# Two of ten first-activation rows of each chunk carried over through DRAM instead of computed again

## What is computed

```
h = jax.nn.relu(_bn(_conv1x1(x, w_pw1), ...)) * mask_dilate
h = h * vector[:, :, None, None]
h = jax.nn.relu(_bn(_dwconv3x3(h, w_dw), ...)) * mask
h = h * vector[:, :, None, None]
h = _bn(_conv1x1(h, w_pw2), ...) * mask
return x + h
```

## Time and profile before

| | |
|---|---|
| median of 3 runs | 1687.53 us (1687.25 to 1690.31) |
| span of the profiled execution, first to last instruction | 1685.9 us |
| TensorE busy | 1588.0 us (94% of the span) |
| ACT busy | 1270.4 us (75%) |
| DVE busy | 1194.2 us (71%) |
| last stage | from 1169.5 us on |
| one chunk of the last stage | 41.0 us |

### The profile page before, as it was taken

How to read it: one execution, slowest core, us unless ns; L and a number is a source line. 1 busy time by engine, 2 the same in 40 slices (tenths; PEclk the granted TensorE clock), 3 DMA queues, 4 the chain that set the end, 5 groups by cost and what they waited for, 6 DMA issues and landing times. The chain is left out here.

```text
span 1685.9 us, 57844 instructions
## 1 busy us (share of the span) xinstructions
PE 1588.0 (94%) x24130; PEld 1254.3 (74%) x24130; DVE 1194.2 (71%) x1993; ACT 1270.4 (75%) x2405; POOL 110.6 (7%) x189
## 2 busy tenths in 40 slices
PE   6999999999999999999999979466999999999996
PEld 5999999999999999999999953114444444454443
DVE  5777777777777777777777758775766666666664
ACT  5888888888888888888888867663666666666663
POOL 4000000000000000000000000000000000000000
PEclk9999999999999999999999999775999999999998
DMA  6656666656666566666666659860134444334334
GB/s 147 166 160 165 171 169 165 164 161 170 169 166 167 160 167 168 165 174 172 164 166 170 170 196 383 326 247 18 43 83 85 88 81 92 81 81 89 83 83 91
DMA packets 96008, 251.53 MB, mean 149 GB/s; under 512 B 22920, under 2 KB 28956, under 8 KB 95772
## 3 DMA queue, kind: packets, MB, share of 16 engines
q1 hardware_dynamic: 84344, 213.56, 43.5%
q0 software_dynamic: 10880, 35.40, 10.6%
q10 hardware_dynamic: 644, 0.49, 0.2%
HBM read 120.74 MB, written 78.79 MB: 118 GB/s over the span
## 5 line engine op out<-in xcount | busy, mean ns | idle before, releaser
L319 PE MATMUL gates<-state,w_high 64*128 64x384 f32 x4608 | 505.9, 338 | 0.0
L319 PEld LDWEIGHTS gates<-state,w_high 64*128 64x128 f32 x4608 | 417.9, 185 | 0.0
L1263 PE MATMUL psd<-shared 32*32 32x384 f32 x10368 | 296.4, 491 | 0.6 <-issue 0.6
L319 PE MATMUL gates<-state,w_low 64*128 64x384 f32 x2304 | 268.3, 338 | 0.0
L1263 PEld LDWEIGHTS psd<-shared 32*32 32x32 f32 x10368 | 164.8, 103 | 131.1 <-issue 77.3
L319 PE MATMUL gates<-x_both,w_high 64*128 64x384 f32 x2304 | 237.3, 338 | 13.8 <-ACT w_high L373 13.8
L378 ACT ACTIVATE sig_f<-gates 48x384 f32<-48x384 f32 x384 | 187.0, 487 | 46.7 <-PE gates L319 41.2
L319 PEld LDWEIGHTS gates<-x_both,w_high 64*128 64x128 f32 x2304 | 207.5, 186 | 13.8 <-ACT w_high L373 13.8
L319 PEld LDWEIGHTS gates<-state,w_low 64*128 64x128 f32 x2304 | 209.4, 186 | 0.0
L1504 DVE SCALAR_TENSOR_TENSOR acc<-shared,acc 128x768 f32<-128x768 f32 x144 | 146.5, 1018 | 75.5 <-ACT acc L1412 71.7
L474 DVE TENSOR_TENSOR h_new<-sig_o,tanh_c 128x384 f32<-128x384 f32 x192 | 107.2, 559 | 122.3 <-ACT tanh_c L396 122.3
(11 more groups left out here) (166 smaller groups left out, 1626.5 us busy)
## 6 DMA issues: line engine op xcount, KB each, us to landing
x_taps<-x_both SPq DMA_DIRECT2D x192, 195.5 KB, 3.2
x_raw<-x_steps SPq DMA_DIRECT2D x192, 192.0 KB, 3.2
h_rows<-h_new SPq DMA_DIRECT2D x136, 192.0 KB, 2.7
h_in<-h_rows SPq DMA_DIRECT2D x34, 768.0 KB, 6.3
x_last<-x_both SPq DMA_DIRECT2D x192, 98.0 KB, 3.0
shared<-x_parts SPq DMA_DIRECT2D x24, 768.0 KB, 9.4
out<-z POOLq DMA_DIRECT2D x47, 336.0 KB, 5.4
x_parts<-x_lanes POOLq DMA_DIRECT2D x48, 288.0 KB, 4.2
```

The source lines that it names most:

```text
L319: return nc.tensor.matmul(gates[p][d][:, m, 0:NH], w[own, n, m, :], moving[own], start=start, stop=stop)
L1263: mm = nc.tensor.matmul(psd[lane:lane + 32, 2 * x + i, 0:NH], wt[own, to:to + 32], h1p[2 * (s % 2) + x][own, dy + 4 * m:dy + 4 * m + 4, dx ...
```

## The change

Each chunk but the first computes eight new rows, in two jobs of four rows. The first two rows of its `h1` come from the chunk before: once a chunk's rows are there, ACT's queue stores its last two rows into a DRAM tensor `halos` (`save`), and when the next chunk's buffer is free, ACT's queue loads them into its first two rows (`back`). The three pairs move as one DMA for two images, the three DVE units as one each: six saves and six loads a chunk, 11 times. New waits: the first taps of a pair on TensorE and `product` on ACT wait for the load (`halo_back`); a load waits for the save (`halo_saved`) and for the buffer; a later `keep` waits until the rows that it overwrites are saved.

```diff
         def span(c, r):
-            first, last = CH * c - 1 + 5 * r, CH * c + 4 + 5 * r
-            lo, hi = max(first, 0), min(last, H)
-            return lo, hi, 5 * r + lo - first
+            lo = CH * c + 1 + 4 * r if c or r else 0
+            hi = min(CH * c + 5 + 4 * r, H)
+            return lo, hi, lo - (CH * c - 1)
...
+        def halo_count(o, c):
+            return 16 * ((NCH - 1) * o + c)
+
+        def halo_rows(c, n, first):
+            at = slice(first * WP, (first + 2) * WP)
+            if n < NP:
+                pair = 2 * ((NP * c + n) % 2)
+                both = shared[:, WCOLS + H1_PX * pair:WCOLS + H1_PX * (pair + 2)]
+                return both.rearrange("p (x n) -> p x n", x=2)[:, :, at]
+            return h1d[(ND * c + n - NP) % 2][:].rearrange("p r w -> p (r w)")[:, at]
+
+        def halo_home(c, n):
+            if n < NP:
+                return halos[c, 2 * n:2 * n + 2].rearrange("x p n -> p x n")
+            return halos[c, len(P_IMAGES) + n - NP]
...
                     if these[0] == 0:
                         pe.wait_ge(relu1_done, 2 * (J + (job(c, k, 1) if s else job_b(0))) + 3)
+                        if c:
+                            pe.wait_ge(halo_back[k], halo_count(o, c))
...
+                def save(c, n):
+                    if c == NCH - 1:
+                        return
+                    j = job(c, n, 1) if n < NP else job(c, DVE_PAIR, 1) if n > NP else job_b(c)
+                    act.wait_ge(relu1_done, 2 * (J + j) + 3)
+                    act.dma_start(halo_home(c, n), halo_rows(c, n, CH)).then_inc(halo_saved[n], 16)
+
+                def back(c, n):
+                    if c == 0:
+                        return
+                    if n < NP:
+                        act.wait_ge(taps_done, PU + NP * c + n)
+                    else:
+                        act.wait_ge(acc_done, D + ND * c + n - NP)
+                    act.wait_ge(halo_saved[n], halo_count(o, c))
+                    act.dma_start(halo_rows(c, n, 0), halo_home(c - 1, n)).then_inc(halo_back[n], 16)
...
                         if r == 0:
                             free(b, c)
+                            if pair != DVE_PAIR and half:
+                                back(c, pair)
+                            if pair == DVE_PAIR and half:
+                                back(c, NP + 2)
...
                     act.wait_ge(relu1_done, 2 * (J + j) + 3)
+                    if c:
+                        act.wait_ge(halo_back[NP + s], halo_count(o, c))
...
                     if c:
                         relu2(c - 1, 2)
+                    save(c, 1)
+                    back(c, NP + 1)
                     relu1(c, DVE_PAIR, 0)
                     relu2p(c, 0, 0)
                     relu1(c, DVE_PAIR, 1)
                     relu2p(c, 0, 1)
+                    save(c, NP + 1)
+                    save(c, NP + 2)
                     product(c, 1, job(c, DVE_PAIR, 1))
...
                     relu2p(c, 1, 0)
+                    save(c, 2)
                     if c + 1 < NCH:
                         relu1(c + 1, FIRST_PAIR, 0)
...
                     if c + 1 < NCH:
+                        save(c + 1, 0)
+                        back(c + 1, NP)
                         relu1_b(c + 1)
                         product(c + 1, 0, job_b(c + 1))
+                        save(c + 1, NP)
```

More of the change, by code:

```diff
@@ L1076, in _, with bottleneck @@
                 program(1)
-def bottleneck(nc, shared, y, out_lanes, packs, passes, mask_rows, masks_stored):
+def bottleneck(nc, shared, y, out_lanes, packs, passes, mask_rows, masks_stored, halos):
     NP, ND, NZ = len(P_IMAGES) // 2, len(D_UNITS), len(GROUPS)
@@ L1119, in bottleneck @@
         pw2_done, zm_done = sem("pw2_done"), sem("zm_done")
+        halo_saved = [sem(f"halo_saved{n}") for n in range(NP + ND)]
+        halo_back = [sem(f"halo_back{n}") for n in range(NP + ND)]
         def par(unit, col):
@@ L1378, in free, with saved @@
                         act.wait_ge(prod_done, D + max(d - 1, 0) + 1)
+                def save(c, n):
[13 more added lines that the diff above has]
+                    act.dma_start(halo_rows(c, n, 0), halo_home(c - 1, n)).then_inc(halo_back[n], 16)
+                def saved(use, per, base):
+                    c, n = divmod(use, per)
+                    if use >= 0 and c < NCH - 1:
+                        act.wait_ge(halo_saved[base + n], halo_count(o, c + 1))
                 def keep(b, c, r, bank):
                     h1 = h1_of(b, c)
+                    if r == 1:
+                        if b in P_IMAGES:
+                            saved(pair_of(b, c) - 2, NP, 0)
+                        else:
+                            saved(ND * c + D_UNITS.index(b) - 2, ND, NP)
                     lo, hi, first = span(c, r)
@@ L1452, in one_pass @@
                 product(0, 0, job_b(0))
+                save(0, 0)
+                save(0, NP)
                 for c in range(NCH):
@@ L1569, in build @@
     x_parts = nc.dram_tensor("x_parts", [X_PARTS, P, X1_PART], F32).ap()
+    halos = nc.dram_tensor("halos", [H // CH, len(P_IMAGES) + len(D_UNITS), P, 2 * WP], F32).ap()
     with ExitStack() as ctx:
@@ L1615, in build @@
             gather(nc, shared, cst, par, w1, place, folded, packs, packs_stored, passes, ident32, half_of)
-        bottleneck(nc, shared, y, out, packs, passes, mask_rows, masks_stored)
+        bottleneck(nc, shared, y, out, packs, passes, mask_rows, masks_stored, halos)
 def kernel(x, L0_conv_w_f, L0_conv_b_f, L0_conv_w_b, L0_conv_b_b, L0_conv_w_proj, L0_conv_gamma, L0_conv_beta,
```

## The result

The changed kernel takes 1677.09 us (median of 4 runs, 1674.32 to 1679.4), the kernel before 1687.39 beside it: a ratio of 0.9941 [0.9926, 0.9955], 10.3 us faster. The forecast was 1671.5, 16 us faster. The wider range of 1668.5 to 1682 holds the result; the forecast's own, 1668.5 to 1675, does not. The profiled execution is the fastest of the four, 1674.32 us with a span of 1672.3. Of the 13.6 us between its span and that of the kernel before, 4.4 lie ahead of the last stage, in code that was not changed: the first taps start at 1172.23 in place of 1176.67. In two later sets the same kernel stood at 0.9949 and 0.9952, so its gain is 8 to 10 us.

What follows compares the result with a forecast made beforehand. The prediction took TensorE to bound the kernel, with ACT about 0.1 us behind it. 1685.9 - 17.3 (rows) + 1.3 (exposed waits) = 1669.9 us of span, the median 1.6 above: 1671.5 us, range 1668.5 to 1682.

Steps and rivals of the forecast that it cites:

- wider range: Whole kernel: 1668.5 to 1682 us, from no exposed wait to beyond the partly exposed issues, held at about 0.8.
- the forecast's own: Whole kernel: the range of 1668.5 to 1675 us if the DMA issues are hidden behind activations, chance 0.58.
- rival A: Four DMA issues on ACT's path a chunk partly exposed, 0.1 to 0.3 us each: about 1680; up to 1684, chance 0.23.
- signs of being wrong by mechanism: In the changed profile: the chunk shortens by less than 1.3 us without 0.3 us gaps at ACT's keeps.
- TensorE's rows: TensorE's jobs: 22 fewer rows, 5 jobs each, at 0.16 us, less 0.3 at the end: 17.3 us gained.
- I take 0.04 us of exposed wait a window: TensorE's taps behind 33 windows wait for ACT, which falls 0.12 us further behind: 1.3 us lost (0 to 4).
- Added on ACT: I take the value near nothing: Twelve DMA issues a chunk on ACT's queue, 0.5 to 0.6 us each, hide behind running activations: near nothing.
- it just fits: Behind the THIRD window: two saves make the product perhaps 0.2 us late, within 0.56 us of room before TensorE needs the keeps.
- DMA ... Nothing: DMA engines: 20 MB more, 46 GB/s beside 83, may delay masks and outputs by some tenths; costs nothing.
- 0.165 us a row-job: TensorE's gain for each row less in a job, taken with no exposed wait for the range's lower end, 1668.5.
- B: Issues serial on ACT in the windows and ahead of THIRD_PAIR's keeps: 2.4 to 3.0 us a chunk, 1697 to 1704, chance 0.10.
- D: A late load or DMA contention holds TensorE or the product: 1 to 3 us a chunk, chance 0.03.

Runs made afterwards that it cites:

- floor: The changed kernel without saves, loads or their waits, and with the jobs of three pairs split into 3 and 5 rows: 1668.82 us, 0.9892.
- short_relu2p: The changed kernel with the second relu2p of each pair, from chunk 1 on, reading 240 of 384 columns: 1676.87 us, 0.9935.
- thin_double: The changed kernel with each save issued twice in a row, all copies 32 bytes a partition in place of 784: 1688.64 us, 1.0013.
- thin: The changed kernel with every save and load kept but moving 32 bytes a partition in place of 784: 1674.56 us, 0.9925.
- no_traffic: The changed kernel without saves, loads or their waits, the carried rows left unfilled: 1673.13 us, 0.9918.
- again: The changed kernel unaltered, run beside the one without copies: 1678.5 us, 0.9949.
- changed_2: The changed kernel unaltered, run on the same chip as the kernels with thin or spread saves: 1677.09 us, 0.9952.
- double_spread: The changed kernel with each save issued twice in full bytes, the second put behind other activations: 1690.67 us, 1.0021.

## Why the prediction was right and where it was wrong

The measured 1677.1 us lies in the wider range and outside the forecast's own, 1668.5 to 1675, which was given 0.58. The wider range reached to 1682 for exposed issues (rival A), and these are not what the result is made of: that it held the result is in part luck. One of the prediction's own signs of being wrong by mechanism was met: the chunk shortens by 1.2 us, less than 1.3, with no gap of 0.3 us between the keeps of a regular window.

- **TensorE's rows** (17.3 us): right. 0.80 us a job, 1.60 us a chunk over the places, and 17.9 us in floor by the medians.
- **"I take 0.04 us of exposed wait a window"**: the mechanism was right, the size wrong. ACT falls as far behind as forecast (0.21 us), but all of the 0.12 us by which it fell further behind is exposed: 0.36 us a chunk, 4.0 us over 11 chunks in place of 1.3. I had held that the second half's first matmul comes 0.45 us later and is covered. short_relu2p shows that it isn't, and the weight loads why: the load for it is due 0.07 us after the run's start, and in the kernel before ACT's last read already ended at 0.04 (median), so there was no slack left. The upper end of that term's range (4) was the answer, +2.7 us.
- **"Added on ACT: I take the value near nothing"**: right in the regular chunk, where an issue is 0.33 to 0.43 us, less than the 0.5 to 0.6 taken. Ahead of the product "it just fits" was too kind by a little: the product waits for ACT's sequencer 4 to 7 times in ten chunks, 1.2 to 2.8 us in all, where one of the issues runs long. The Trainium skill, Perfetto Trace Analysis, "DMA Instruction — HWDGE (DVE, Sync)", has the sequencer held until the push is done, and this kernel's runs agree: thin_double, 66 more issues of 32 bytes a partition, is 14 us slower than thin. At two issues in a row that cost almost nothing.
- **"DMA ... Nothing"**: this is the step that failed. The average share (0.56) and the landings (2.7 us for the pairs' loads, 4.7 for a unit's) never made TensorE wait for a load, as forecast. What I did not price is that other transfers, which no line of the kernel issues, share the engines. no_traffic against again puts 5.4 us on the copies as a whole, thin against changed_2 2.5 us on their bytes (4.6 by the ratios, whose intervals just overlap). That the cost is paid in TensorE's pauses is measured; the way from the bytes to the pauses is open.
- **The sum by what was measured**: 17.3 - 4.0 = 13.3, less some 5 for the copies, 8 to 9; measured 10.3, 7.7 and 8.9 in three sets.
- **Slips in the working.** By its own terms the lower end of the range, no exposed wait and 0.165 us a row-job, is 1669.7 and not 1668.5. TensorE waited for ACT in two more places than the earlier trace rows shows, 0.6 and 0.2 us. Neither changes the forecast.
- **The rivals.** A's number (1680) was near, but not its mechanism: the issues are not exposed by 0.1 to 0.3 us each. B's mechanism exists and turns the sign, if narrowly, where each save is issued twice (thin_double, 1.0013). D was right in kind (contention), not in place: it was not a late load.

## What to carry to other kernels

A DMA issued from ACT's queue cost next to nothing here where the activations already handed over last longer than the issues in a row (2 x 0.35 to 0.45 us under 1.24 us) or where ACT has time anyway; count the row and its place, not the sum over a chunk. Where two engines run side by side, work taken from the one that bounds can expose the other by the whole difference, so price it in full unless a row shows slack, and look for that slack in the weight loads, which run ahead of the matmuls. And when a change trades computation for DMA bytes in a long unrolled program, look for what the bytes cost TensorE in pauses that no semaphore explains, some 2 to 5 us for 20 MB here.

## What the hardware did that I had not expected

- TensorE pauses of 0.38 to 2.4 us from matmul to matmul in the midst of runs of independent matmuls, all 75 of them ending 1.2 to 1.7 us after the end of an instruction packet. The packets themselves take no longer with more traffic (median 0.96 us before, 1.01 in double_spread), but those ahead of a pause start late, 6.7 us after their predecessor in place of 4.8; what holds them up is open.
- The 17th weight load of a tap run starts 0.07 us after the first where nothing holds it, while 16 matmuls at the mean of 28 ns take 0.45 us: a wait for a bank is met that much earlier than the matmuls say.
- An issue on ACT's sequencer takes 0.33 to 0.45 us, but now and then 1.0 to 2.7.
- The place of the issues and the bytes were worth about the same, 14 us each: 66 further DMA instructions of some 0.4 us in the wrong place cost as much as 66 with their 10 MB do in better ones.
